# A decoder layer rebuilt as a pipeline of three chains, with folded norms and attention chunks of 64

## The chip, the cores and the metric

The kernel is written in Bass and runs on one core of one Trainium2 chip. The metric is the device time of one execution in microseconds, as a median of runs. TensorE (PE) multiplies matrices, VectorE (DVE), ScalarE (ACT) and GpSimd (POOL) work on tiles of 128 partitions, SyncE (SP) starts transfers. Each engine executes its own list of instructions in order; semaphores tie the lists together.

## The reference, cut to what matters

Everything is fp32; there are 4 batches of 256 tokens and 256 features.

```python
# attention, 16 heads of 16; the decay of a head h is r_h
h1 = layernorm(x)
q, k, v = rotary(h1 @ Wq), rotary(h1 @ Wk), h1 @ Wv
# chunks of 128 tokens, state kv of 16 x 16 per head
inter  = (q * r**(i + 1)) @ kv
intra  = ((q @ k.T) * dmask) @ v
kv     = r**128 * kv + (k * r**(127 - i)).T @ v
x1 = x + rms_norm(inter + intra, rms_w) @ Wo
# similarity with a context of 256 x 64
kv_c = ctx @ W_k.T + b_k                       # 256 x 64
sim  = (layernorm(x1) @ kv_c) @ kv_c.T / 16     # 256 x 256
x2   = x1 + softmax(layernorm(sim, eps=1e-6) * gamma + beta)
# mixture of 8 experts of 256 x 256, the best 2 by the router
h3  = layernorm(x2)
out = x2 + sum_e gate_e * (h3 @ We[e] + be[e])
```

The decay `r**n` makes chunks of any length exact: a chunk of 64 with one more state between the chunks gives the same sums.

## The kernel before, in words

A batch is worked through in three stages, all with two tiles of 128 tokens. The *front*: norm 1, transposes, the products for q, k, v, the rotation, masked scores, attention, projection, x1. The *back*: norm 2, the two products with the context keys, norm of the similarities, softmax, x2, norm 3, router logits, gates. The *experts*: eight units of a tile and two experts each (`expert_unit`, six fp32r products of 512 columns from a high and a low part of each operand), and VectorE adds each expert's product, weighted by its gate, to `acc` (`add_units`).

`passes` runs six bodies: body i has the front of batch i, the back of batch i-1 and the experts of batch i-2. Bodies 2 and 3 have all three stages and are a loop. The order of the instructions in a body is written out by hand on each engine. All products of two fp32 tiles appear in the trace as two records; fp32r products and transposes as one.

- `scores(t)`: four products of 64 rows and 512 columns for a tile. The queries are laid out in four masked copies (`qx`, made by `head_queries` on ScalarE), and VectorE multiplies each bank by the decay (`decay_scores`).
- `attend(t)`: for each head one product of 32 output rows and 128 columns, `probs` with `vpad`; for tile 1 also `state` with `qd`.
- `state_product`: one state, between the two chunks of 128.
- A norm is statistics and an aggregate on VectorE, a power of -0.5 on GpSimd (`rsqrt`), and a subtraction with multiplication on VectorE (`ln_apply`), before the transposes on TensorE.
- `keep_clock(n, ...)`: n products with the identity whose result nobody reads, 18 in all: at the start, in bodies 0 and 1, and in body 4 while the last back stage runs.
- `route`: some twenty small VectorE instructions from logits to gates.

## Time and profile before

| | |
|---|---|
| median of 3 runs | 174.38 us (174.18 to 174.51) |
| profiled execution, its own time | 174.52 us |
| its span | 172.3 us |
| TensorE busy | 152.0 us, 88% |
| VectorE busy | 123.4 us, 72% |
| ScalarE busy | 61.5 us, 36% |
| GpSimd busy | 32.2 us, 19% |

The span is what the profiler sees from the first to the last instruction; the time of an execution is 2.2 us longer. Busy time adds the intervals in which an engine has an instruction under way. Matmuls overlap in their pipeline, so a group of them can be shorter than its count times the mean of one.

### The profile page before, as it was taken

The numbers are of one execution on the slowest core, as the hardware profiler recorded it, in microseconds if no ns is written. First come the engines' busy times: TensorE is split into PE (matmuls) and PEld (weight loads), VectorE is DVE, ScalarE is ACT, GpSimd is POOL, SyncE is SP. The second block draws the span as 40 slices with busy tenths as digits, with TensorE's granted clock in tenths as the row PEclk, the third lists the DMA queues.
The fourth block names the chain that finished last, engine by engine and source line by source line (L and its number), as shares of the span: only waits on it lengthen the run. The fifth ranks groups of instructions, "written<-read, shape, count | busy, mean of one in ns | idle before, by whom it ended". The sixth has DMA issues, their size and how long they took to land.

```text
span 172.3 us, 3040 instructions
## 1 busy us (share of the span) xinstructions
PE 152.0 (88%) x981; PEld 104.0 (60%) x981; DVE 123.4 (72%) x401; ACT 61.5 (36%) x171; POOL 32.2 (19%) x53
## 2 busy tenths in 40 slices
PE   0999999799779899999779899998698899998991
PEld 0555458257436778678248787675376667636880
DVE  0523593887899889757899597668996557877762
ACT  3265846055850320537712202469203120410100
POOL 4103200314320032045200130423100204010030
PEclk9999999999999999999999999999999999999998
DMA  5999400002000000000040000000100000001001
GB/s 150 313 351 348 104 0 4 0 4 76 0 4 0 0 4 0 2 0 0 0 122 22 0 0 0 0 0 0 61 0 0 2 0 0 0 0 61 4 0 61
DMA packets 7930, 7.29 MB, mean 42 GB/s; under 512 B 2264, under 2 KB 7664, under 8 KB 7792
## 3 DMA queue, kind: packets, MB, share of 16 engines
q1 hardware_dynamic: 7424, 6.79, 12.6%
q10 hardware_dynamic: 496, 0.37, 0.8%
q8 instruction: 6, 0.10, 0.2%
q14 instruction: 4, 0.03, 0.1%
HBM read 6.11 MB, written 1.05 MB: 42 GB/s over the span
## 4 chain that ended last, share of the span: by engine, by line
PE 49%; DVE 27%; issue 7%; ACT 6%; DVEq 5%; DMA 2%; POOL 2%
PE bank L793 13%; PE ebank L793 12%; DVE probs L624 7%; PE ebank L801 4%; PE bank L841 4%; ACT qx L426 3%; DVE stats L520 2%; PE bank L923 2%; DMA cst<-in_consts 2%; PE bank L881 2%; PE bank L808 2%; DVE w_e_lo L585 2%; DVEq L521 2%; DVE norm L531 2%; POOL rs L326 2%
## 5 line engine op out<-in xcount | busy, mean ns | idle before, releaser
L624 DVE TENSOR_TENSOR probs<-bank,dec 128x512 f32<-128x512 f32 x32 | 19.8, 680 | 1.6 <-PE bank L881 1.6
L326 POOL TENSOR_TENSOR rs<-ve,nhalf 128x2 f32<-128x2 f32 x16 | 12.1, 756 | 37.1 <-DVE ve L525 37.0
L881 PE MATMUL bank<-qx,kT 64*128 64x512 f32 x64 | 18.0, 624 | 0.8 <-ACT kv L481 0.8
L801 PE MATMUL ebank<-cst 128*128 128x512 f32 (+1 forms) x22 | 11.5, 645 | 4.7 <-DMA cst<-in_consts 4.7
L558 DVE SCALAR_TENSOR_TENSOR acc<-ebank,gate,acc 128x256 f32<-128x256 f32 x26 | 11.3, 477 | 3.2 <-PE ebank L793 3.0
L793 PE MATMUL ebank<-w_e_hi,h3T_hi 128*128 128x512 f32 x40 | 13.4, 416 | 0.2 <-DVE w_e_lo L585 0.2
L426 ACT ACTIVATE qx<-bank,cst 128x256 f32<-128x256 f32 x32 | 12.6, 487 | 0.0
L558 DVE SCALAR_TENSOR_TENSOR acc<-bank,gate,acc 128x256 f32<-128x256 f32 x22 | 9.3, 478 | 4.5 <-PE bank L793 3.0
L793 PE MATMUL ebank<-w_e_hi,h3T_lo 128*128 128x512 f32 x40 | 12.5, 394 | 0.0
L793 PE MATMUL ebank<-w_e_lo,h3T_hi 128*128 128x512 f32 x40 | 12.4, 392 | 0.0
L326 POOL TENSOR_TENSOR rms_rs<-rms_ve,nhalf 128x2 f32<-128x2 f32 x4 | 3.1, 785 | 46.1 <-DVE rms_ve L768 46.1
L347 POOL TENSOR_TENSOR rot_b<-qk,cst 128x128 f32<-128x128 f32 x16 | 7.8, 505 | 19.7 <-ACT qk L400 19.7
L881 PEld LDWEIGHTS bank<-qx,kT 64*128 64x128 f32 x64 | 7.2, 185 | 6.4 <-issue 2.2
L337 POOL TENSOR_TENSOR acc<-acc,biases 128x512 f32<-128x512 f32 x4 | 5.1, 1286 | 30.2 <-DVE acc L558 30.2
L394 ACT COPY pT<-bank 128x256 f32<-128x256 f32 x8 | 2.7, 375 | 21.7 <-PE bank L808 21.7
L434 ACT ACTIVATE sqT<-bank 128x256 f32<-128x256 f32 x8 | 3.1, 383 | 18.2 <-PE bank L906 16.5
L801 PEld LDWEIGHTS ebank<-cst 128*128 128x128 f32 x22 | 4.3, 213 | 8.7 <-DMA cst<-in_consts 4.6
L906 PE MATMUL bank<-probs,vpad 128*32 128x128 f32 x256 | 9.2, 275 | 0.0
L923 PE MATMUL bank<-w_o,attT 128*128 128x256 f32 x32 | 8.9, 400 | 0.0
L808 PE MATMUL bank<-cst,norm 128*128 128x128 f32 x36 | 6.4, 301 | 2.6 <-DVE norm L531 2.5
L793 PEld LDWEIGHTS ebank<-w_e_lo,h3T_hi 128*128 128x128 f32 x40 | 7.5, 188 | 1.7
L793 PEld LDWEIGHTS ebank<-w_e_hi,h3T_lo 128*128 128x128 f32 x40 | 7.5, 188 | 1.7
(137 smaller groups left out, 321.4 us busy)
## 6 DMA issues: line engine op xcount, KB each, us to landing
w_e<-in_L_ffn_We SPq DMA_DIRECT2D x2, 1024.0 KB, 9.8
xin<-in_x SPq DMA_DIRECT2D x4, 256.0 KB, 3.8
dec<-in_decay SPq DMA_DIRECT2D x1, 1024.0 KB, 6.6
out<-outb SPq DMA_DIRECT2D x8, 128.0 KB, 1.7
cst<-in_consts ACTq DMA_DIRECT2D x1, 282.0 KB, 3.9
w_qkv<-in_L_attn_Wq SPq DMA_DIRECT2D x1, 256.0 KB, 4.4
w_qkv<-in_L_attn_Wk SPq DMA_DIRECT2D x1, 256.0 KB, 4.9
w_qkv<-in_L_attn_Wv SPq DMA_DIRECT2D x1, 256.0 KB, 5.1
```

The costliest lines, as they stand in the source:

```text
L326: nc.gpsimd.tensor_tensor(dst[:], src[:], nhalf[:], ALU.pow).then_inc(done, 1)
L347: nc.gpsimd.tensor_tensor(rot_b[:, t, :, a, :], v[:, :, 1 - a, 0:ROT], sin, ALU.mult).then_inc(s_rb, 1)
L426: o = act.activation(qx[:, t, :, k, :], bank[t][:, 0:D].rearrange("p (g n) -> p g n", g=GROUPS), ACT.Copy, scale=cst[:, C_PICK + k:C_PICK ...
L558: nc.vector.scalar_tensor_tensor(out=outb[:, t, :] if last else acc[:, t, :], in0=expert_bank(b, u)[:, (e % 2) * D:(e % 2 + 1) * D], scala ...
L624: nc.vector.tensor_tensor(probs[:, t, 4 * n:4 * n + 4, :], bank[2 + n][:].rearrange("p (h n) -> p h n", h=4), dec[:, 4 * n:4 * n + 4, :], ...
L793: mm = pe.matmul(dst, a[ka][:, c, a_cols], b[kb][:, c, b_cols], start=(n == 0 and c == 0), stop=(n == 2 and c == KC - 1))
L801: pe.matmul(dst[:, 0:cols], ident, cst[:, 0:cols], start=True, stop=True)
L808: mm = pe.transpose(banks[t][:, c * P:(c + 1) * P], norm[n][:, t, c * P:(c + 1) * P], ident)
L841: mm = pe.matmul(dst, h1T_full[:, c, cols], w_qkv[:, c, w_cols], start=(c == 0), stop=(c == KC - 1))
L881: pe.matmul(bank[2 + n][:], kT[rows, t, g, :], qx[rows, t, g, :, :], start=True, stop=True).then_inc(s_sc_ps, 1)
L906: mm = pe.matmul(bank[t][32 * q:32 * q + 32, g * P:(g + 1) * P], vpad[:, t, h, :], probs[:, t, h, :], start=(par == 0), stop=(par == 1 and ...
L923: mm = pe.matmul(bank[2 + t][:, 0:D], attT[:, t, g, :], w_o[:, g, :], start=(g == 0), stop=(g == GROUPS - 1))
```

## The change

The program is reordered and four things are computed in another way.

- **Order.** There is no loop over bodies any more. After the fronts of batches 0 and 1 and the chain of batch 0, there are bodies b = 1 to 3. A body has: attention, projection, similarity and softmax of batch b; the transposes, logits, routing and all eight expert units of batch b-1; and q, k, v, rotation, scores and states of batch b+1. The products for q, k and v of batch b+1 stand ahead of six of the eight expert units. After body 3 come the experts of batch 3. `xin`, `cin` have a buffer for each batch, `vpad`, `qd`, `state`, `kvT`, `kv`, `x2`, `h3T` have two.
- **Chunks of 64.** `scores` makes 16 products a tile of 32 rows by 64 columns of the array, with 128 columns of data; `qx` has two copies, not four; `decay_scores` reads two tiles of 128x512 per tile. `states` makes three states a batch by 32 products of 32 columns. `attend` handles both tiles: 64 products with `probs` and 24 with `state`, of 64 columns each.
- **Folded norms.** x is only centered ahead of the transposes; the factor `rs1` is applied as q, k and v leave their bank. Norm 2 is not applied at all: the centered context keys and one variance stand for it (`context_sums`, `center_x1`, `square_similarities`, `sim_variance`). Norm 3 is applied through the gates (`gate_y`), with its mean in `x1c` and its sum of squares from `square_x2` on ScalarE.
- **Dummy products.** Three calls of `keep_clock` with 256 columns at the start are left.

The core of the diff. `-` lines of the old bodies are cut; each new function shown is new or rewritten.

```diff
 @block.gpsimd
+            for b in range(B):
+                if b == 0:
+                    for t in range(TILES):
+                        rotary_cross(1, t)
+                if b + 2 < B:
+                    x_rstd(b + 2)
+                rms_rstd(b)
+                if b == 0:
+                    keys_for_states(1)
+                x1_variance(b)
+                if 0 < b < LAST:
+                    for t in range(TILES):
+                        rotary_cross(b + 1, t)
+                sim_rstd(b)
+                if 0 < b < LAST:
+                    keys_for_states(b + 1)
+                if b:
+                    add_biases(b - 1)
+                x2_rstd(b)
 @block.scalar
+            def center_x1(b, t):
+                act.wait_ge(s_nmu3, b + 1)
...
+                act.activation(x1c[:, t], x1[:, t], ACT.Identity, bias=nmu3[:, t:t + 1]).then_inc(s_x1c, 1)
+                act.activation(squares1[:, t], x1[:, t], ACT.Square, bias=nmu3[:, t:t + 1],
+                               accum_out=ssq1[:, t:t + 1]).then_inc(s_sq1, 1)
...
+            queries_keys(1, 0)
+            attention_out(0, 0)
+            attention_out(0, 1)
+            queries_keys(1, 1)
+            high_experts(1, 0)
+            head_queries(1, 0)
...
+            negate_beta()
+            context_transposed(1)
+            context_sums(1)
+            context_centered(1)
+            context_keys(1)
+            softmax_exp(0, 0)
+            softmax_exp(0, 1)
...
+            for b in range(1, B):
+                for t in range(TILES):
+                    x2_transposed(b - 1, t)
+                for t in range(TILES):
+                    square_x2(b - 1, t)
+                attention_out(b, 0)
+                attention_out(b, 1)
+                gate_exponent(b - 1)
+                if b < LAST:
+                    center_x(b + 1, 0)
+                    center_x(b + 1, 1)
+                gates_transposed(b - 1)
+                expert_biases(b - 1)
+                for t in range(TILES):
+                    x1_transposed(b, t)
+                if b < LAST:
                     for t in range(TILES):
+                        x_transposed(b + 1, t)
+                keys_product(b)
+                center_x1(b, 0)
+                center_x1(b, 1)
+                if b < LAST:
+                    context_transposed(b + 1)
+                    values(b + 1, 0)
+                    values(b + 1, 1)
+                square_similarities(b, 0)
+                square_similarities(b, 1)
+                if b < LAST:
+                    context_sums(b + 1)
+                    context_centered(b + 1)
+                    queries_keys(b + 1, 0)
+                    context_keys(b + 1)
+                    queries_keys(b + 1, 1)
+                    head_queries(b + 1, 0)
+                softmax_exp(b, 0)
+                softmax_exp(b, 1)
+                if b < LAST:
+                    head_queries(b + 1, 1)
 @block.vector
+            rotate(1, 0)
+            low_experts(0)
+            rms_variance(0)
+            residual1(0)
...
+            for b in range(1, B):
+                x2_low(b - 1, 0)
+                x2_low(b - 1, 1)
+                if b == 1:
                     low_experts(1)
+                if b + 2 < B:
+                    x_stats(b + 2)
+                route(b - 1)
+                rms_variance(b)
+                residual1(b)
+                add_experts(b - 1, 0)
+                if b < LAST:
+                    x_low(b + 1, 0)
+                    x_low(b + 1, 1)
+                sim_variance(b)
+                if b < LAST:
+                    rotate(b + 1, 0)
+                softmax_input(b)
+                if b < LAST:
+                    rotate(b + 1, 1)
+                    decay_queries(b + 1, 0)
+                add_experts(b - 1, 1)
+                residual2(b, 0)
+                residual2(b, 1)
+                if b < LAST:
+                    decay_queries(b + 1, 1)
+                    decay_scores(b + 1, 0)
+                    decay_scores(b + 1, 1)
+                add_experts(b - 1, 2)
+                if b < LAST:
+                    mask_states(b + 1)
+                add_experts(b - 1, 3)
 @block.tensor
+            def states(b):
...
+                for t, v, n in ((0, 0, 0), (0, 1, 1), (0, 2, 2), (1, STATES, 2)):
                     for g in range(GROUPS):
+                        for q in range(PAIRS):
...
+                            mm = pe.matmul(qk_bank(b, 0)[32 * q:32 * q + 32, at:at + 2 * DH],
+                                           kd[:, v, g * P + 32 * q:g * P + 32 * q + 32], pair,
...
+            def scores(b, t):
...
+                for n in range(2):
...
                     for g in range(GROUPS):
+                        for c in range(HALVES):
+                            half = slice(c * CH, (c + 1) * CH)
+                            for r in (2 * n, 2 * n + 1):
+                                rows = slice(32 * r, 32 * r + 32)
+                                mm = pe.matmul(chain[half, r, g * P:(g + 1) * P], kT[rows, t, g, half],
+                                               qx[rows, t, g, :, half], start=True, stop=True)
+            def attend(b):
...
+                            for c in range(HALVES):
+                                half = slice(c * CH, (c + 1) * CH)
+                                for q in range(PAIRS):
+                                    pe.matmul(chain[32 * q:32 * q + 32, c, cols],
+                                              vpad[b % 2][half, t, g * 8 + q * 2 + par, :], probs[half, t, q, at],
...
+                for n in range(STATES):
...
+                        for q in range(PAIRS):
+                            rows = slice(32 * q, 32 * q + 32)
+                            mm = pe.matmul(chain[rows, c, cols], state[b % 2][rows, n * GROUPS + g, :],
+                                           qd[b % 2][rows, t, g, c * CH:(c + 1) * CH], start=False,
+            def project(b, t):
...
+                if t:
+                    pe.wait_ge(s_rv, b + 1)
+            def expert(b, q, t):
...
+                elif b < LAST or q in (0, QS - 1):
+                    before = TILES * E * b + 4 * (q - 1) + 3 + t
...
+                    pe.wait_ge(s_exd, before)
+            for b in range(1, B):
+                transpose_x2(b - 1, 0)
+                transpose_x2(b - 1, 1)
+                attend(b)
+                logits(b - 1)
+                expert(b - 1, 0, 0)
+                square_sums(b)
+                project(b, 0)
+                project(b, 1)
+                transpose_gates(b - 1)
+                expert(b - 1, 0, 1)
+                bias_product(b - 1)
+                transpose_x1(b, 0)
+                transpose_x1(b, 1)
+                if b < LAST:
+                    transpose_x(b + 1, 0)
+                    transpose_x(b + 1, 1)
+                keys_product(b)
+                if b < LAST:
+                    transpose_context(b + 1)
+                    project_v(b + 1, 0)
+                    project_v(b + 1, 1)
+                similarities(b)
+                if b < LAST:
+                    context_product(b + 1)
+                    project_qk(b + 1, 0)
+                    project_qk(b + 1, 1)
+                    transpose_keys(b + 1)
+                expert(b - 1, 1, 0)
+                if b < LAST:
+                    transpose_qk(b + 1, 0)
+                expert(b - 1, 1, 1)
+                if b < LAST:
+                    transpose_qk(b + 1, 1)
+                expert(b - 1, 2, 0)
+                if b < LAST:
+                    scores(b + 1, 0)
+                    scores(b + 1, 1)
+                expert(b - 1, 2, 1)
+                if b < LAST:
+                    states(b + 1)
+                expert(b - 1, 3, 0)
+                expert(b - 1, 3, 1)
```

## Rows read from the trace of the kernel before

**Rows 1.** The page's table of busy time (us, share of the span, instructions).

```profile
PE 152.0 (88%) x981; PEld 104.0 (60%) x981; DVE 123.4 (72%) x401; ACT 61.5 (36%) x171; POOL 32.2 (19%) x53
```

**Rows 2.** Timeline of TensorE at attention: start us, length us, engine, line, operation.

```profile
55.30 1.52 PE L906 MATMUL bank<-probs,vpad 128*32 128x128 f32 x48
...
91.78 1.52 PE L906 MATMUL bank<-probs,vpad 128*32 128x128 f32 x48
...
93.11 0.40 PE L911 MATMUL bank<-qd,state 128*32 128x128 f32 x8
...
93.33 0.65 PE L906 MATMUL bank<-probs,vpad 128*32 128x128 f32 x14
...
94.23 0.61 PE L919 MATMUL bank<-onescol,sqT 128*128 128x1 f32 x4
...
127.73 1.52 PE L906 MATMUL bank<-probs,vpad 128*32 128x128 f32 x48
```

**Rows 3.** Windows: stretch, length; busy us (count) by engine, granted clock, DMA.

```profile
55.30:91.78 36.48, 33.29 (x240) 24.62 (x239) 29.99 (x100) 13.47 (x40) 7.78 (x11) 1.00 0.06 17
...
91.78:127.73 35.95, 33.01 (x239) 24.55 (x238) 28.88 (x98) 13.46 (x40) 7.39 (x11) 1.00 0.02 8
...
169.00:172.30 3.30, 0.00 (x0) 0.00 (x0) 1.05 (x3) 0.00 (x0) 0.00 (x0) 0.79 0.24 79
```

**Rows 4.** Chain of work that ended last: start us, us, what.

```profile
22.36 0.44 PE bank L890 x4
...
22.81 1.92 PE bank L881 x8
...
30.66 0.89 DVE x L776 x2
...
36.24 0.59 PE bank L957 x8
...
101.14 2.75 PE bank L793 x12
...
150.71 0.50 DVE x L617
```

**Rows 5.** Timeline of TensorE, products of `keep_clock`.

```profile
4.65 2.93 PE L801 MATMUL ebank<-cst 128*128 128x512 f32 x4 [4.65 <-DMA cst<-in_consts]
...
16.75 1.98 PE L801 MATMUL ebank<-cst 128*128 128x512 f32 x4
```

**Rows 6.** Groups of weight loads by shape: busy us, mean ns, idle before.

```profile
L911 PEld LDWEIGHTS bank<-qd,state 128*32 128x32 f32 x64 | 2.3, 110 | 0.0
...
L957 PEld LDWEIGHTS bank<-pT,kv 128*64 128x64 f32 x32 | 1.7, 136 | 0.9 <-issue 0.9
...
L890 PEld LDWEIGHTS bank<-vpad,kd 128*128 128x128 f32 x16 | 2.2, 191 | 0.5 <-issue 0.5
```

**Rows 7.** Timeline of VectorE: routing, four additions, the last additions.

```profile
93.32 0.18 DVE L632 TENSOR_REDUCE lg<-ebank 128x16 f32<-128x32 f32 x1
...
96.10 0.18 DVE L665 TENSOR_TENSOR gate_parts<-gate,gate_parts 128x16 fp32r<-128x16 f32 x1
...
146.05 1.66 DVE L558 SCALAR_TENSOR_TENSOR acc<-ebank,gate,acc 128x256 f32<-128x256 f32 x4
...
169.19 0.86 DVE L558 SCALAR_TENSOR_TENSOR outb<-ebank,gate,acc 128x256 f32<-128x256 f32 x2
```

**Rows 8.** Timeline of ScalarE: copies of queries, a pass with a sum.

```profile
114.60 0.22 ACT L418 ACTIVATION_READ_ACCUMULATOR ez<-zb,nmax 128x1 f32 x1
...
116.71 1.58 ACT L426 ACTIVATE qx<-bank,cst 128x256 f32<-128x256 f32 x4
```

**Rows 9.** The page's costliest groups, VectorE and GpSimd: busy us, mean ns.

```profile
L624 DVE TENSOR_TENSOR probs<-bank,dec 128x512 f32<-128x512 f32 x32 | 19.8, 680 | 1.6 <-PE bank L881 1.6
...
L326 POOL TENSOR_TENSOR rs<-ve,nhalf 128x2 f32<-128x2 f32 x16 | 12.1, 756 | 37.1 <-DVE ve L525 37.0
...
L347 POOL TENSOR_TENSOR rot_b<-qk,cst 128x128 f32<-128x128 f32 x16 | 7.8, 505 | 19.7 <-ACT qk L400 19.7
```

1506 lines of the change are left out of this document (798 added, 708 removed).

## The prediction

> **What bounds the kernel now.** I read the page's busy table first [rows 1]: TensorE is busy for 152.0 of 172.3 us, VectorE for 123.4. Then the places where one product recurs, the attention product `probs x vpad`: it starts at 55.30, 91.78 and 127.73 us [rows 2]. So the span falls into four stretches: 55.3 us until the second batch attends, two bodies of 36.5 and 36.0, and 44.6 to the end. The windows cut at these points [rows 3] say what fills a body: 33.3 and 33.0 us of TensorE, 30.0 and 28.9 of VectorE, 13.5 of ScalarE. A body is TensorE's work plus 3 us of holes. The chain of waits changes hands between TensorE and VectorE all the way [rows 4]. A change that shortens norms on VectorE, ScalarE or GpSimd gains little in a body unless TensorE's own time falls too, so I count TensorE first.
>
> **TensorE's work in one body.** An fp32 product is two records in the trace, an fp32r product one.
> Weight loads of 32, 64 and 128 columns last 110, 136 and 190 ns [rows 6]: 26 or 27 ns more for each 32 columns, on a fixed 83. I read this as loads that stream one after the other, 27 ns per 32 columns. The pace of the small products fits: 48 records of 128 columns run from 91.78 to 93.11, 27.7 ns each, and 8 records of the state product until 93.33, 27.5 ns each [rows 2].
> - `attend` now takes 80 records in 2.45 us (91.78 to 94.23) [rows 2]. After: 64 products with `probs` and 24 with `state`, 176 records. The columns per record halve (64 for 128), the weight loads double. At 27.5 ns: 4.84 us, +2.4.
> - `states` replaces 4 records of 0.44 us in all [rows 4] by 32 products, 64 records: 1.76 us, +1.3.
> - `scores`: now 16 records, 1.92 us a tile [rows 4], 3.84 a batch. After: 64 records a batch, each with a 64-column load, 53 ns by the step of [rows 6]: 3.4 us, -0.4. The nearest row with such loads, the key product, took 0.59 us for 8, 74 ns each [rows 4]: 4.7 us, +0.9. I take 53, as the four tiles of the array are all distinct.
> - q, k, v, expert units (2.75 us for two [rows 4]), context and routing products are the same instructions in other places: 0.
>
> Sum: 33.2 + 3.3 = 36.5 us of TensorE in a body, already its whole present length. The floor of the unseen cost is that time goes with columns alone: half of 27.6, 13.8 ns a record. That would make attend 2.4, states 0.9 and scores (half of 3.84) 1.9 us: 31.7 in all. The ceiling is the key product's 74 ns for scores. The nearest rows to `attend` and `states` are at 27.5, with the same 32-column loads, so I take that.
>
> The Trainium skill speaks to this (TensorE: Matmul & The Clock Gate, "Wait — 56ns, not 53.3ns?"): start-to-start of matmuls never falls below about 25 ns, however few columns. By it attend would be 4.4 us (an estimate), not 4.84, and halving the columns buys nothing. No run here yet shows 64-column records.
>
> **What leaves the other engines.** Masked scores: 4 of 0.68 us a tile become 2, about -2.5 us on VectorE [rows 9]; `qx` 4 copies a tile become 2, -1.5 us on ScalarE (four in 1.58 [rows 8]). The norms lose statistics and normalizing passes on VectorE and return as ScalarE passes with a sum (`center_x1`, `square_similarities`, `square_x2`, `context_sums`): some 0.36 us back to back plus 0.22 for a sum [rows 8]. VectorE falls to about 26 us a body, ScalarE rises from 13.5 [rows 3] to about 20. Neither is the bound as a sum. They matter as links of the chain.
>
> **The chain through a body after.** I count from the start of `transpose_x2(b-1)` on TensorE, in each queue's new order.
> 1. Transposes to 0.5, attend to 5.35, `logits` to 6.6, one expert unit to 8.0.
> 2. `route(b-1)` starts at 6.65 and takes 3.0 us now [rows 7] plus 0.2 for `gate_y`: 9.8. `rms_variance(b)` is queued behind it on VectorE: 9.95. GpSimd's root 0.8 [rows 9], `residual1` 0.89 [rows 4]: x1 at 11.7. `project(b, 1)` waits for `rms_variance` as well.
> 3. TensorE goes through projection, gates, the second expert unit, bias: 13.0; x1 transposed 13.45. ScalarE is then busy without a break: biases, pT and h1T 15.05, pkvT 15.35, `center_x1` 17.2, ctxT 17.6, values 18.5, squares 19.7, context 21.05, q and k of both tiles 22.6.
> 4. `sim_rstd(b)` is behind both `rotary_cross(b+1, t)` on GpSimd. The second needs q and k of tile 1: 22.6 + 1.0 + 0.8 [rows 9] = 24.4, 4.7 us after the squares were done. `softmax_input` to 26.3; `rotate(b+1, 1)` is queued behind it: 27.1. So `transpose_qk(b+1, 1)` leaves TensorE idle for about 2 us.
> 5. `add_experts(b-1, 1)` to 29.0 (four in 1.66 [rows 7]), x2 at 30.35. Expert unit (2,0) waits for its bank until 28.6. Then scores 1.7 and 1.8, expert unit, states 1.8, two expert units: 39.5.
>
> A body is thus 39.5 us: TensorE's 34 or so by sum of steps, and 5.5 of holes. Now: 36.2 on the mean.
>
> **Before the bodies.** The first product starts 0.6 us earlier (no root ahead of the centred x). From there the front of batch 1 is laced into batch 0's. `attend(0)` ends at about 33.5. `low_experts(0)` on VectorE needs `high_experts(1, 0)`, which ScalarE does only after `attention_out(0)`, and `rms_variance(0)` is queued behind it: x1 of batch 0 at about 39.5, now 31.55 [rows 4]. In exchange the second front is nearly through. `softmax_input(0)` waits for `negate_beta` on ScalarE, scores of batch 1 for `context_keys(1)`. The second attend starts at 55.6; now 55.3. No gain.
>
> **The end.** Batch 3 attends, with the eight units of batch 2 as filler. Expert unit (2,0) waits from 18.8 to 22.5 for `add_experts(2, 1)`, queued behind `softmax_input(3)`. x2(3) is ready at 24.25, 23.75 after attend's start (now 23.5 [rows 2, 4]), but its transposes are queued behind three more units: 28.1. Then, without a third norm ahead of them, transposes, parts and logits to 31.3. Eight units and routing to 43.0, last addition 44.2, and 2.25 us from there to the end as now (170.05 to 172.3 [rows 7]): 46.5. Now 44.6 [rows 2].
>
> **Sum.** 55.6 + 39.5 + 39.5 + 46.5 = 181.1 us; the profiled execution took 174.52 for a span of 172.3, so 2.2 lie outside: 183.3. The median of the runs is 0.14 below the profiled one. I say 183.
>
> **The rivals.**
> - *Small products at array pace (0.20).* Two row halves and four column groups abreast would put a 64-column record at 13.8 ns. 896 small records lie on the path (176 + 64 at the start, 240 in each body, 176 at the end): 896 x 13.7 = 12.3 us less, and about 3.0 less for scores: 168.0, faster. It decides where 8.8 us are won: 3.0 on scores and a pace of 21 ns. For it: half the columns. Against: the stepping load time [rows 6] and that 32 columns of weights never went faster than 27 ns [rows 2]. The Trainium skill (TensorEngine Tiling, "Theoretical Speedup") promises up to 16 times for both dimensions small, which is this case's best end.
> - *The lacing hides the holes (0.12).* Expert units absorb steps 4 and 5, and a body is its 36.5 us of work: 6 less, 177.3; with 3 to 5 more from the start, 172 to 175.
> - *The clock falls (0.13).* The first four dummy records (two of 512 and two of 256 columns) took 2.93 us, four of 512 later 1.98, so the first ran at the lower of the two levels, 1.2 and 2.4 GHz [rows 5]; and with TensorE idle over the last 3.3 us the granted clock averaged 0.79 [rows 3]. The change leaves 3 of the 18 dummy calls. TensorE is nearly idle from about 46 to 54 us, and for 3.7 us in the last body. At half clock for some 5 us behind each: 3 more at the end, 2 more at the start, 188.
> - *The forecast itself (0.55)*: 177 to 187.
>
> **Numbers.** Faster by over 0.2% (about what this kernel's runs can tell from no change): the first rival's 0.20 and 0.05 of the second's, 0.25. Within: 0.03. Slower: 0.72. The range takes in the floor of the small records and the clock case: 168 to 190; the forecast's own range is 177 to 187.
>
> **What would show it.** Right: 64-column records 25 to 28 ns apart; attend near 4.8 us; its starts 39 to 40 us apart; `sim_rstd` ending GpSimd's wait after the rotary terms; TensorE waiting for `rotate(b+1, 1)`; `rms_variance(0)` behind `low_experts`. Wrong: attend under 3 us; a body under 36; the second attend before 50 us; a granted clock of half after the holes.

## The result, and the profile after

The changed kernel takes 184.49 us (median of four runs, 183.99 to 185.95); the kernel before took 174.44 beside it. The ratio is 1.0583, with an interval from 1.0515 to 1.0651: slower. The forecast was 183.0. Some executions of the kernels below ran at a lower mean clock than others of the same kernel; the intervals leave them out and the medians don't, so where the two part, single runs are given.

The total fits. It does not follow that its terms do, so I go through the trace in the order in which the forecast was made. First the page of the changed kernel: busy time by engine, two of its rows by slices (a digit is the busy share, or the granted clock in tenths, of a fortieth of the span), and the queue that loads instructions (packets, MB, share).

```profile
PE 144.8 (79%) x1767; PEld 108.8 (60%) x1767; DVE 96.1 (53%) x322; ACT 73.7 (40%) x228; POOL 38.0 (21%) x70
...
PE   1996696976269989947999989577978974779991
...
PEclk9999579579855999996699999975699999696999
...
q8 instruction: 14, 0.23, 0.5%
```

TensorE has less to do than before (144.8 us for 152.0 in [rows 1]), though part of it ran at the lower clock, and VectorE is 22% lighter. Neither bounds the kernel: TensorE is idle for 37 us of 182. The row of the clock has seven dips, each with or just behind a slice in which TensorE's digit is 7 or less.

The windows, cut at the attentions as in [rows 3] (stretch, length; busy us and count for PE, PEld, DVE, ACT, POOL; granted clock; DMA), then seven short ones:

```profile
0.00:55.50 55.50, 39.10 (x551) 27.87 (x552) 24.00 (x73) 28.98 (x78) 14.58 (x32) 0.82 0.33 100
55.50:95.03 39.53, 34.32 (x443) 26.20 (x442) 24.60 (x81) 16.37 (x55) 9.41 (x15) 0.87 0.01 2
95.03:133.78 38.75, 34.41 (x443) 26.09 (x442) 21.49 (x72) 16.51 (x55) 8.06 (x14) 0.87 0.03 8
133.78:182.20 48.42, 36.92 (x333) 28.64 (x332) 26.06 (x99) 11.81 (x43) 5.95 (x9) 0.93 0.05 17
44.00:48.00 4.00, 0.68 (x6) 0.29 (x2) 1.33 (x5) 3.22 (x10) 0.88 (x2) 1.00 0.00 0
80.00:84.00 4.00, 2.31 (x10) 1.63 (x10) 3.93 (x11) 1.72 (x5) 1.84 (x2) 0.91 0.01 4
116.00:120.00 4.00, 1.22 (x8) 0.55 (x6) 3.97 (x13) 2.22 (x8) 2.10 (x4) 1.00 0.00 0
152.00:156.00 4.00, 2.20 (x7) 1.78 (x8) 3.93 (x12) 1.10 (x4) 1.29 (x1) 0.86 0.00 0
83.20:90.10 6.90, 5.98 (x73) 4.14 (x72) 5.08 (x10) 0.00 (x0) 0.86 (x1) 0.51 0.01 2
49.10:59.30 10.20, 7.58 (x238) 6.06 (x239) 7.53 (x17) 4.53 (x15) 1.55 (x2) 0.50 0.01 2
120.80:131.00 10.20, 9.28 (x141) 6.51 (x140) 6.71 (x14) 0.00 (x0) 0.97 (x1) 0.50 0.01 2
```

The stretches are 55.5, 39.5, 38.8 and 48.4 us, where the forecast had 55.6, 39.5, 39.5 and 46.5. But the bodies of before ran at a granted clock of 1.00 throughout [rows 3], and these at 0.87. In the last three windows it is half, 1.2 of 2.4 GHz, and two of the three begin within 1.1 us of the end of a window in which TensorE was busy for only 0.68 and 1.22 of 4 us (48.0 to 49.1, 120.0 to 120.8); the third begins inside one with 2.31 (83.2).

Next the small products, on TensorE's timeline (start us, length us, line, operation, records). The third attention is at the full clock, the second at half of it; the last shows a stop:

```profile
55.50 2.04 PE L1176 MATMUL chain<-probs,vpad 64*32 64x64 f32 x128
57.48 1.29 PE L1185 MATMUL chain<-qd,state 32*32 32x64 f32 x40
59.31 0.31 PE L1185 MATMUL chain<-qd,state 32*32 32x64 f32 x8 [0.55 <-issue]
...
90.57 0.76 PE L1106 MATMUL front<-vpad,kd 128*32 128x32 f32 x64
...
95.03 1.48 PE L1176 MATMUL chain<-probs,vpad 64*32 64x64 f32 x128
96.45 0.87 PE L1185 MATMUL chain<-qd,state 32*32 32x64 f32 x48
...
133.78 1.48 PE L1176 MATMUL chain<-probs,vpad 64*32 64x64 f32 x128
135.20 0.52 PE L1185 MATMUL chain<-qd,state 32*32 32x64 f32 x20
137.09 0.64 PE L1185 MATMUL chain<-qd,state 32*32 32x64 f32 x28 [1.37 <-issue]
```

From 95.03 to 96.45, where the next form begins, 128 records take 1.42 us: 11 ns each, not the forecast's 27.5. At half the clock it is 15.5 ns (55.50 to 57.48). The states' 64 records take 0.76 us, 12 ns. Attention as a whole lasts 2.2 us at the full clock (95.03 to 97.25), where the forecast had 4.84: the largest term of its count for TensorE was wrong by more than a factor of two. In the first body, at half the clock and with a stop, the same attention still took 4.1 us (55.50 to 59.56).

What stood in its place? The waits of step 4, in the first body, are there (an entry in brackets is idle time before the instruction, and what ended it):

```profile
73.15 0.16 DVE L850 SCALAR_TENSOR_TENSOR sim_ve<-ssq,ve 128x2 f32<-128x2 f32 x1 [3.75 <-ACT squares_sim L586]
...
75.07 0.99 POOL L363 TENSOR_TENSOR rot_b<-qk,cst 128x128 f32<-128x128 f32 x2 [3.68 <-ACT qk L494]
...
76.40 0.82 POOL L363 TENSOR_TENSOR rot_b<-qk,cst 128x128 f32<-128x128 f32 x2 [0.33 <-ACT qk L494]
...
77.17 0.69 POOL L348 TENSOR_TENSOR sim_rs<-sim_ve,nhalf 128x2 f32<-128x2 f32 x1
...
78.00 0.88 DVE L859 SCALAR_TENSOR_TENSOR zg<-chain,sim_rs,gam 128x256 f32<-128x256 f32 x2 [1.40 <-POOL sim_rs L348]
...
80.92 0.66 PE L1090 MATMUL front<-cst,qk 128*128 128x128 f32 x4 [2.07 <-DVE qk L794]
...
82.74 1.60 DVE L873 SCALAR_TENSOR_TENSOR x<-ez,rsum,x1c 128x256 f32<-128x256 f32 x1
82.78 1.28 POOL L409 TENSOR_TENSOR acc<-acc,biases 128x512 f32<-128x512 f32 x1 [1.21 <-DVE acc L943]
```

`sim_ve` is ready at 73.3 and GpSimd begins its root at 77.17, behind the cross terms of both tiles; TensorE then stands idle 2.07 us for `rotate(2, 1)`. The same hole comes again at 118.62 (2.05 us). The clock falls at 83.2, 2.3 us after the first of them ended, and at 120.8, 2.2 us after the second. The last two lines were in nobody's forecast: VectorE's x2 instruction takes 1.60 us instead of 0.48 while GpSimd adds the biases.

### The profile page after: what moved, and what is told of

The parts are those of the page before. It is cut to its first block, busy times and chain, and to the rows that moved or that the text cites. A ratio compares the mean times of both kernels' runs of the same rounds, so it can differ in the third digit from the quotient of the medians.

```text
span 182.2 us, 4515 instructions
## 1 busy us (share of the span) xinstructions
PE 144.8 (79%) x1767; PEld 108.8 (60%) x1767; DVE 96.1 (53%) x322; ACT 73.7 (40%) x228; POOL 38.0 (21%) x70
## 4 chain that ended last, share of the span: by engine, by line
PE 59%; ACT 14%; issue 10%; DVE 9%; POOL 3%; DMA 2%; POOLq 1%; DVEq 0%; ACTq 0%
PE ebank L1037 24%; PE chain L1205 5%; PE chain L1158 5%; PE chain L1176 3%; DVE acc L943 2%; PE chain L1185 2%; ACT squares_x L575 2%; PE front L1257 2%; PE chain L1195 2%; PE front L1044 2%; POOL rot_b L363 2%; DMA cst<-in_consts 2%; ACT qx L516 2%; PE front L1029 2%; PE chain L1025 2%
## 5 line engine op out<-in xcount | busy, mean ns | idle before, releaser
L1037 PE MATMUL ebank<-w_e_hi,h3T_hi 128*128 128x512 f32 x56 | 22.2, 481 | 5.3 <-DVE acc L943 4.6
L943 DVE SCALAR_TENSOR_TENSOR acc<-ebank,gate_y,acc 128x256 f32<-128x256 f32 x40 | 17.4, 478 | 11.3 <-PE ebank L1037 11.3
L1037 PE MATMUL ebank<-w_e_lo,h3T_hi 128*128 128x512 f32 x56 | 20.2, 445 | 0.0
L1037 PE MATMUL ebank<-w_e_hi,h3T_lo 128*128 128x512 f32 x56 | 19.7, 437 | 0.0
L1037 PEld LDWEIGHTS ebank<-w_e_hi,h3T_hi 128*128 128x128 f32 x56 | 10.3, 216 | 9.2 <-DVE acc L943 6.1
L1158 PE MATMUL chain<-qx,kT 32*64 32x128 f32 x256 | 10.8, 429 | 3.5 <-DVE probs L826 3.1
L826 DVE TENSOR_TENSOR probs<-chain,dec 128x512 f32<-128x512 f32 x16 | 10.3, 686 | 5.9 <-PE chain L1158 5.9
L1158 PEld LDWEIGHTS chain<-qx,kT 32*64 32x64 f32 x256 | 7.8, 213 | 6.5 <-issue 6.5
L372 POOL TENSOR_TENSOR kd<-qk,cst 128x256 f32<-128x256 f32 x16 | 10.0, 644 | 5.6 <-DVE qk L794 5.6
L1205 PE MATMUL chain<-w_o,attT 128*128 128x256 f32 x32 | 10.3, 467 | 0.0
L873 DVE SCALAR_TENSOR_TENSOR x<-ez,rsum,x1c 128x256 f32<-128x256 f32 x8 | 7.2, 905 | 0.3
```

The lines of the kernel that those rows point to most:

```text
L372: o = nc.gpsimd.tensor_tensor(kd[:, n].rearrange("p (h d) -> p h d", h=H), qk[:, t, D:].rearrange("p (h d) -> p h d", h=H), kdec[:, v].uns ...
L826: nc.vector.tensor_tensor(probs[:, t, rows], chain[:, rows, 0:D], dec[:, rows], ALU.mult).then_inc(s_sc, 1)
L873: nc.vector.scalar_tensor_tensor(out=x2[b % 2][:, t, :], in0=ez[:, t], scalar=rsum[:, t:t + 1], in1=x1c[:, t, :], op0=ALU.mult, op1=ALU.ad ...
L943: nc.vector.scalar_tensor_tensor(out=outb[:, t, :] if last else acc[:, t, :], in0=expert_bank(b, q, t)[:, (e % 2) * D:(e % 2 + 1) * D], sc ...
L1037: mm = pe.matmul(dst, a[ka][:, c, a_cols], b[kb][:, c, b_cols], start=(n == 0 and c == 0), stop=(n == 2 and c == KC - 1))
L1158: mm = pe.matmul(chain[half, r, g * P:(g + 1) * P], kT[rows, t, g, half], qx[rows, t, g, :, half], start=True, stop=True)
```

## Experiments

The theory after the result: the holes of step 4, of the start and of the end cost twice, once as idle time and once more because the clock falls behind them; the small products are cheap, and their price has nothing to do with the time. Rivals: the holes alone; the small products after all; the supply of instructions, that is TensorE standing still until its next instructions have been loaded.

**1. Fill the holes.** TensorE computes products that nobody reads (512 columns of fp32 into a free bank; two records, 0.96 us), 19 of them in the places where it waits. Nothing else changes.

```
+            def fill(n, dst=None):
+                for _ in range(n):
+                    pe.matmul((chain[:, 2] if dst is None else dst)[:, 0:512], ident, w_qkv[:, 0, 0:512],
+                              start=True, stop=True)
...
                 if b < LAST:
+                    fill(2)
                     transpose_qk(b + 1, 1)
+                else:
+                    fill(3)
                 expert(b - 1, 2, 0)
```

> The changed kernel with dummy products (identity times a weight tile, 512 columns, 0.43 us a record at the full clock) in the holes of TensorE: before transposes and scores that wait, in the stretch before the second attend, and in the last body; nobody reads their result. Theory clock: the changed kernel ran TensorE at 1.2 GHz for about 48 of 182 us, behind its holes, and the pieces of work in these stretches took some 14 us longer than the same pieces elsewhere; with the holes filled the mean granted clock is above 0.97 and the time falls from 184.5 to 172 to 177. Rival waits: the low clock costs only time in which TensorE would wait anyway; the clock rises but the time stays within 182 to 185.

Measured: median 174.20 (172.50 to 176.77), ratio to before 0.99 (0.986 to 0.9939); the runs behind the ratio took 172.6 and 172.5 us, at a mean clock of 0.987 and 0.990, where the changed kernel has 0.869. With 18 us of work added it is 12 us faster than the changed kernel, and 1% faster than the kernel before. The clock rival had the right cause. The supply of instructions is not what was won back: the stops with no releaser inside the attentions add up to 3.4 us in this version's trace (1.88 and 1.54) and to 3.5 in the changed kernel's (1.57, 0.55 and 1.37).

**2. Take two waits out of the queues.** GpSimd takes the root of the similarity's variance ahead of the cross terms; VectorE does the softmax's input ahead of both rotations.

```
+                sim_rstd(b)
                 if 0 < b < LAST:
                     for t in range(TILES):
                         rotary_cross(b + 1, t)
-                sim_rstd(b)
...
-                if b < LAST:
-                    rotate(b + 1, 0)
                 softmax_input(b)
                 if b < LAST:
+                    rotate(b + 1, 0)
                     rotate(b + 1, 1)
```

> The changed kernel with GpSimd's root for the similarities ahead of the rotary terms of the next batch, and VectorE's softmax input ahead of both rotations. Theory order (step 4 of the prediction): in bodies 1 and 2 the softmax input starts at once behind the squares instead of 4.7 us later, the hole of 2 us before the transposes of q and k of tile 1 goes or halves; 178 to 182, of it 2 to 3 us for each body, if the clock stays as it is. Rival: the rotation is now late instead, the hole moves to the transposes of tile 0, and the time stays within 183 to 186.

Measured: median 175.18 (174.29 to 181.96), ratio 1.0033 (0.9993 to 1.0074), 9.3 us under the changed kernel. The expectation was too small, since it priced the idle time alone. The root now begins 0.1 us after its input (timeline of this version):

```profile
74.50 0.16 DVE L850 SCALAR_TENSOR_TENSOR sim_ve<-ssq,ve 128x2 f32<-128x2 f32 x1 [3.74 <-ACT squares_sim L586]
74.74 0.69 POOL L348 TENSOR_TENSOR sim_rs<-sim_ve,nhalf 128x2 f32<-128x2 f32 x1 [2.00 <-DVE sim_ve L850]
```

The mean clock rose to 0.931: with the hole of each body smaller, the two clock falls in the bodies did not come. Two short moves are worth nearly as much as the dummy work.

**3. Both.** The edits of 1 and 2 together.

> Both edits. If clock and order are separate costs, the gains add: 167 to 173, below the kernel before. If the hole was the cause of the low clock, the sum is less than the parts: 172 to 176.

Measured: median 170.03, ratio 0.9655 (0.9596 to 0.9714), from runs of 169.05 and 167.52. The time lies in the range that the expectation gives for gains that add, but that range was built on smaller gains. Those measured, 11.9 and 9.3, would add up to 163.3; they don't add, since both take back the same clock. The orders are worth some 4 us on top of the filling. Windows of this version:

```profile
0.00:52.31 52.31, 40.52 (x567) 25.42 (x568) 23.95 (x73) 29.16 (x80) 14.56 (x32) 1.00 0.36 106
52.31:89.53 37.22, 34.66 (x448) 25.96 (x448) 25.19 (x81) 15.73 (x54) 9.69 (x15) 0.95 0.01 2
89.53:123.63 34.10, 33.09 (x449) 24.60 (x448) 21.89 (x72) 16.23 (x55) 8.53 (x14) 1.00 0.03 10
123.63:167.30 43.67, 37.82 (x343) 28.08 (x342) 25.89 (x99) 11.77 (x43) 5.94 (x9) 0.99 0.06 19
```

A body at the full clock is 34.1 us, two short of the 36.0 of before. TensorE is busy for 33.1 of them, of which three dummies are 2.9: the body's own work is about 30.2 us. This version is the base of what follows.

**4. The small products twice.** On the changed kernel the state products are issued two times, 64 records more in each of four batches.

```
-                for t, v, n in ((0, 0, 0), (0, 1, 1), (0, 2, 2), (1, STATES, 2)):
+                for t, v, n in ((0, 0, 0), (0, 1, 1), (0, 2, 2), (1, STATES, 2)) * 2:
```

> The changed kernel with the 32 products of the states issued twice for each batch (the second set repeats the first): 64 records more a batch, three of the four batches on the path. By the prediction's price of 27.5 ns a record: 3 x 1.76 = 5.3 us more, 189.8. By the pace that the trace of the changed kernel shows for its small products, 11 to 16 ns: 3 x 0.7 to 1.0 = 2 to 3 us more, 186.5 to 187.5. Rival supply: long runs of small instructions stop TensorE for 0.5 to 1.6 us each, put down to issue, and more of them give more such stops: 188 or more at an unchanged pace between the stops.

Measured: median 183.66 (182.46 to 187.6), ratio 1.0514 (1.0468 to 1.056): no rise, where all three expectations had one.

```profile
25.40 1.48 PE L1106 MATMUL front<-vpad,kd 128*32 128x32 f32 x128
...
42.97 1.20 PE L1106 MATMUL ebank<-vpad,kd 128*32 128x32 f32 x116
45.89 0.32 PE L1106 MATMUL ebank<-vpad,kd 128*32 128x32 f32 x12 [1.73 <-issue]
```

128 records in 1.48 us: 11.6 ns, so the forecast's pace is refuted a second time. A stop of 1.73 us with no releaser has appeared inside them, where the changed kernel has none; with those inside the attentions the stops add up to 6.0 us, for 3.5. So the supply rival is right about the stops. It is wrong about the time, because the mean clock is higher (0.906): TensorE ran at half clock for 34 us instead of 48. I have not tested why.

**5. The start.** On the base of 3: ScalarE converts `high_experts(1, 0)` before `attention_out(0)`, GpSimd takes the RMS root before `x_rstd(2)`, VectorE does `sim_variance(0)` before `decay_queries(1, 1)`, and the context's copy goes ahead of a conversion.

```
+            high_experts(1, 0)
             attention_out(0, 0)
             attention_out(0, 1)
             queries_keys(1, 1)
-            high_experts(1, 0)
...
             rotate(1, 1)
-            decay_queries(1, 1)
             sim_variance(0)
+            decay_queries(1, 1)
             softmax_input(0)
```

> Base: the version with filled holes and the new queue orders (median 170.03 us, its profiled run 169.05, attentions at 26.1, 52.3, 89.5 and 123.6 us). Theory: ahead of the loop three more waits are only waits in queues: `rms_variance(0)` stands on VectorE behind a `low_experts` piece that waits 4.12 us for ScalarE's `high_experts(1, 0)`, so that `project(0, 1)` waits 1.35 us; `sim_variance(0)` stands behind `decay_queries(1, 1)`, which comes 1.4 us after the squares are ready; and the context's copy stands on ScalarE behind a 1.06 us conversion. With all three moved, the second attention should start 2 to 3 us sooner (49.3 to 50.3) and the median be 167 to 168. Rival: TensorE stops for its instructions in the attention products anyway (1.87 and 1.53 us there); if that supply is what bounds this stretch, the stops grow by what the waits lose, and the time stays within 1 us (169 to 171).

Measured: four runs of 166.06, 168.1, 171.26 and 171.64, at mean clocks from 0.996 down to 0.956 (the base: 167.52 to 171.79). In the two profiled runs, 169.05 and 166.06, the second attention starts 1.6 us sooner (50.69) and the third and fourth 3.0 sooner (86.51, 120.62): 1.6 from the waits, less than expected, and 1.4 because the clock fall of the base behind its second attention (56.9 to 60.3 us) did not come. The stops in the attentions stayed at 1.87 and 1.54 us, so the rival falls, but with runs 2 us apart the gain in time is not settled by this experiment alone.

**6. The last body.** On the base of 3: an expert unit in place of a dummy in front of `keys_product`, the additions of unit pairs 1 and 2 ahead of the softmax and of x2, the gates transposed two units sooner at the end. All five dummies of the last body and behind it are out.

```
-                if b == LAST:
-                    fill(1)
+                if b == LAST:
+                    expert(b - 1, 1, 0)
                 keys_product(b)
...
+                if b == LAST:
+                    add_experts(b - 1, 1)
                 sim_variance(b)
                 softmax_input(b)
```

> Same base (170.03). Theory: the end is long because in the last body the expert units are queued where they wait for VectorE's additions, and these stand behind the softmax; the fills (four of 0.5 us) and the waits before `expert(2, 2, 0)` and `expert(2, 3, 0)` (0.86 and 1.40 us) go, and the 1.3 us by which VectorE waits for the biases at the end. With the units in the gaps, the additions ahead of the softmax, and the gates transposed two units sooner, the end from the last attention (43.7 us in the base) should be 38 to 40, the median 165 to 167. Rival: the last x2 becomes late (the softmax now stands behind four additions, 1.7 us, and GpSimd's addition of the biases falls on it), and TensorE waits before its transposes with a hole long enough to lower the clock: 168 to 171.

Measured: median 167.35 (166.19 to 167.61), ratio 0.9574 (0.9494 to 0.9653). The end is 42.4 us from the last attention, not 38 to 40: the rival came in part. (The expectation also counts a dummy at 0.5 us; it lasts 0.96.) Two lines say where the rest went:

```profile
138.51 1.27 DVE L943 SCALAR_TENSOR_TENSOR acc<-ebank,gate_y,acc 128x256 f32<-128x256 f32 x3 [2.82 <-PE ebank L1040]
...
149.03 0.36 PE L1260 MATMUL front<-w_r_hi_lo,h3T_hi 128*128 128x16 f32 x2 [1.78 <-DVE h3T_lo L881]
```

The additions delay `sim_variance` to 139.69, and TensorE waits 1.78 us for the low part of x2, queued behind four additions more.

**7. q, k, v behind two of the units.** On the base of 3, this undoes the lead of q, k and v that the section on the change describes: in bodies 1 and 2 the next batch's context product, q, k and key transposes come after units (1, 0) and (1, 1).

```
                 similarities(b)
+                expert(b - 1, 1, 0)
+                expert(b - 1, 1, 1)
                 if b < LAST:
                     context_product(b + 1)
                     project_qk(b + 1, 0)
                     project_qk(b + 1, 1)
                     transpose_keys(b + 1)
-                expert(b - 1, 1, 0)
-                if b < LAST:
                     transpose_qk(b + 1, 0)
-                expert(b - 1, 1, 1)
```

> Same base (170.03): in bodies 1 and 2 the next batch's context product, q and k, and key transposes stand behind the units (1, 0) and (1, 1), that is ahead of four expert units instead of six. This undoes, on this base, the last phrase of the change's name. If the lead is needed: the way from q, k to the next attention (copy 0.69, cross terms 0.76, rotation 0.43, transposes, 1.2 us of copies, scores, two decays of 1.3) no longer hides behind the four units of 5.6 us that are left, and each of the two bodies grows by 1 to 3 us: 172 to 176. Rival: the lead is not needed, as the softmax and x2 set the next attention's start: 169.5 to 170.5.

Measured: median of ten runs 175.57 (172.56 to 181.35), ratio 0.9953 (0.989 to 1.0017) against the base's 0.9655, so 3% or some 5 us slower. The second body, at the full clock in both, is 36.2 us (94.42 to 130.59) against 34.1; the first, 42.6 against 37.2, also has a stretch of 10 us at half clock. So the lead itself is worth 2.1 us a body, and the rest of the 5 comes with the clock. The lead is needed, and it is a gain of the change that the total hides.

**8. The biases apart.** On the base of 3, GpSimd's addition of the biases waits until both tiles of x2 are written.

```
                 pool.wait_ge(s_exd, TILES * E * b + 8)
+                if b < LAST:
+                    pool.wait_ge(s_x2, TILES * (b + 2))
```

> Base: the version with filled holes and new queue orders (170.03; its profiled run 169.05). GpSimd's addition of the expert biases (1.29 us) waits until both tiles of x2 are written, instead of running while VectorE computes the first. Theory: the two engines hold each other up when both work on SBUF alone: VectorE's x2 instruction, 1.61 us while the addition runs, comes down to 0.48 in all three bodies; the addition then falls on the decays of the scores, which read PSUM, and if these are held up as well (0.43 more or up to 1.2 more in each body) nothing is won: 168 to 171. Rival: the 1.6 us have another cause (the length of a wait inside the record, the operands of x2 itself): x2 stays at 1.6 us with no GpSimd work beside it, and the time rises by the wait for the biases, 171 to 173.

Measured: 169.46 to 174.63, median 173.5, where the base has 167.52 to 171.79: nothing won that these runs could show, as three of the four ran at a mean clock of 0.970 or less. But the mechanism shows in the trace. The first group of the base, the second of this version (busy us, mean ns):

```profile
L873 DVE SCALAR_TENSOR_TENSOR x<-ez,rsum,x1c 128x256 f32<-128x256 f32 x8 | 7.3, 908 | 0.3
```

```profile
L828 DVE TENSOR_TENSOR probs<-chain,dec 128x512 f32<-128x512 f32 x16 | 10.3, 684 | 3.9 <-PE chain L1159 3.9
...
L875 DVE SCALAR_TENSOR_TENSOR x<-ez,rsum,x1c 128x256 f32<-128x256 f32 x8 | 3.9, 485 | 0.3
```

All eight x2 instructions now last 0.48, without GpSimd beside them. In the first body GpSimd's addition (85.24 to 86.52) lies beside `qd`, which reads PSUM and takes its usual 0.49 for two. So the holding up goes with instructions of VectorE that have both inputs in SBUF. It is not on the path in the second body, which is at the full clock in both versions: 34.11 us here (94.53 to 128.64) and 34.10 in the base.

**9. A rest inside attention.** On the base of 3, two dummy products stand between the 128 and the 48 small products of each attention.

```
+                fill(2)
                 for n in range(STATES):
                     t, c = divmod(n + 1, HALVES)
```

> Same base (170.03): two dummy products of 512 columns (0.94 us) stand in each of the four attentions between the 128 products with probs and the 48 with the states. The base has stops of 1.87 and 1.53 us with no releaser in the first two attentions' state products and none in the last two. If such a stop is TensorE running out of instructions that are being fetched, time in which it works on few long instructions lets the fetch catch up: the two stops shrink by about 0.9 us each, the last two attentions get 0.9 us longer, and the sum is near 170 to 172. Rival: the stop has another cause that goes with the place (a wait that the trace doesn't name): both stops stay at 1.5 to 1.9 us, and the whole is 3.8 us longer, 173 to 174.

Measured: median 171.69 (171.35 to 172.22), ratio 0.9849 (0.9775 to 0.9923). The second attention of the base, then of this version:

```profile
52.31 1.47 PE L1175 MATMUL chain<-probs,vpad 64*32 64x64 f32 x128 [0.43 <-issue]
53.72 0.54 PE L1184 MATMUL chain<-qd,state 32*32 32x64 f32 x24
55.79 0.54 PE L1184 MATMUL chain<-qd,state 32*32 32x64 f32 x24 [1.53 <-issue]
```

```profile
52.28 1.48 PE L1175 MATMUL chain<-probs,vpad 64*32 64x64 f32 x128 [0.43 <-issue]
53.68 1.98 PE L1294 MATMUL chain<-w_qkv,cst 128*128 128x512 f32 x4
55.60 0.87 PE L1185 MATMUL chain<-qd,state 32*32 32x64 f32 x48
```

The two rests last 1.92 us (53.68 to 55.60), twice what the expectation says. Both stops, 1.87 and 1.53 us, are gone, and the last two attentions, which had none, are 1.9 and 1.8 longer. That is what instructions on their way would do: the stop vanishes when the engine is given something long to do in the meantime, which a wait tied to the place would not. It wins nothing, since 1.92 us of work replaced 1.87 of standing still, and the second attention starts at 52.28 for 52.31.

The packed traces settle it. They hold each packet of the instruction queue q8 (16 KB) with its time. In the changed kernel packets landed at 29.58, 57.97 and 135.70 us, and TensorE resumed at 30.93, 59.31 and 137.09, that is 1.35, 1.34 and 1.39 us later. It is the same in all 25 stops of 0.5 us or more inside runs of small records in these traces: TensorE resumes 1.20 to 1.57 us after a packet has landed. In the third attention of the changed kernel (95.03 to 97.25) no packet lands, and there is no stop.

**10. All of it.** Prologue as in 5; rests in the first two attentions; and in the last body two unit pairs on free banks, two additions ahead of the softmax instead of four, the low part of x2 before the last additions.

```
+            if b == LAST - 1 and q == 2 or b == LAST and q == 1:
+                return chain[:, 1 + t]
+            if b == LAST and q in (0, 3):
+                return chain[:, 3 * t]
+            return ebank[t]
...
+                if b < LAST:
+                    add_experts(b - 1, 3)
             x2_low(LAST, 0)
             x2_low(LAST, 1)
+            add_experts(LAST - 1, 3, 0, 2)
             route(LAST)
+            add_experts(LAST - 1, 3, 2, 4)
```

> Both edits that measured a gain on the base, with the last body's miss mended. The prologue's orders gave 3 us of the profiled run; the rests of 0.94 us between the 128 and the 48 small products go only into the first two attentions, where they took away stops of 1.87 and 1.53 us. In the last body four additions no longer stand ahead of `sim_variance` (1.2 us late before) nor ahead of `x2_low` (TensorE waited 1.78 us for it); two expert units there and two of the last batch write to free banks, so that they wait for no addition. Expected: the end from the last attention 38 to 40 us where the base has 43.7 and the first version of this edit 42.4; the other three stretches 24 + 35.5 + 34; in all a median of 160 to 164. Rival: VectorE, with some 15 us of additions, routing and one 1.3 us wait for GpSimd behind the last x2, now sets the end and it stays at 41 or more: 164 to 167.

Measured: median 162.17 (161.58 to 163.28), ratio 0.9286 (0.9218 to 0.9354): 7% faster than the kernel before. Its last three stretches:

```profile
51.61:87.81 36.20, 35.17 (x452) 25.28 (x453) 25.00 (x81) 15.26 (x51) 9.23 (x15) 1.00 0.01 2
87.81:121.91 34.10, 33.08 (x449) 24.54 (x449) 21.87 (x72) 16.26 (x55) 8.55 (x14) 1.00 0.03 10
121.91:161.50 39.59, 34.24 (x333) 26.34 (x332) 25.75 (x99) 11.88 (x43) 5.95 (x9) 1.00 0.06 21
```

The end is 39.6 us, in the expected range, and the rival, with 41 or more, did not come.

**11. Without the rests.** As 10, with the rests and one dummy of the start taken out and the context's keys and the exponentials ahead of a conversion on ScalarE.

> Base: the version with all edits (median 162.17 us; profiled run 163.28, attentions at 25.96, 51.61, 87.81, 121.91 us). A rest of two dummy products turned out to last 1.92 us, as much as the stop that it replaced (1.87 and 1.53 us), so the rests should have won nothing. Without them the stops should come back at about their old length and the time stay within 0.5 us on that account. The other edit is in the stretch before the second attention: one of the three dummy products ahead of the context product goes (0.96 us), and ScalarE copies the context's keys and takes the exponentials ahead of a 1.03 us conversion, behind which TensorE waited 0.86 us. Expected from this: the second attention 1 to 1.8 us sooner. In all 160 to 161.5. Rival: the hole in front of the context product is only as long as the dummy work made it and the clock falls behind the shorter filling: 162 to 164.

Measured: profiled run 159.88, the fastest execution of all, with the second attention at 48.56 for 51.61: 3 us sooner, more than the 1 to 1.8 expected, as the clock fall at 46.4 to 49.8 us of version 10 is gone too. The stops are back at 1.49 and 1.44. But the six runs spread from 159.88 to 165.58 (median 163.19, ratio 0.9341, 0.9288 to 0.9395), their mean clock from 1.000 down to 0.955. The same program holds its clock in some executions and not in others, as version 3 did (0.987 down to 0.966); whether the missing filling is the reason is not tested. The median is no better than that of 10, and which of the two is faster stays open.

## Why the prediction came out right, and where it was not

The time, 183 for 184.49, and the sign were right. The argument was half right. Its terms, in its own order:

- **Attend, states, scores.** Mis-sized, and the largest error. Attend lasts 2.2 us, not 4.84; states 0.76, not 1.76; scores 0.65 and 1.1 for the two tiles (timeline of version 3), 1.75 and not 3.4. For four attentions and three of the others that is 10.6 + 3.0 + 5.0 = 18.6 us too much. The step that failed was the reading of [rows 6] as loads that stream one after the other, 27 ns per 32 columns. It fails for the old shape of the load too: the records of `states` have tiles of 128 rows by 32 columns, as the 27.5 ns records of [rows 2] had, and run 12 ns apart. What they have less of is data, 32 columns for 128, so the 27.5 ns were not the price of the load. The first rival, small products at array pace, had 13.8 ns; measured are 11 to 12, in the changed kernel and in version 4, and 17 on the tiles of 32 x 32. It had the right mechanism and the wrong result, 168.0, because it left the clock and the waits as they were. The Trainium skill (TensorE: Matmul & The Clock Gate, "Wait — 56ns, not 53.3ns?") gives 25 ns as the least distance between two starts; for records of 64 columns on tiles of 64 x 32 and 32 x 32 it does not hold here, and the measured 11 and 17 ns decide. The prediction also has two sums for TensorE's work in a body, 36.5 us and "34 or so by sum of steps", and does not reconcile them. Measured, without dummies and at the full clock, it is 30.2 (version 3), near the 31.7 that it gave as the floor.
- **The chain through a body** looks right in the first body, to within about a microsecond at every point that I compared. From the start of the x2 transposes at 54.42 us, x1 came at 11.0 (forecast 11.7), the variance of the similarities at 18.7 (squares 19.7), `rotate(b+1, 1)` at 26.4 (27.1), x2 at 30.5 (30.35), the next transposes at 40.1 (39.5). The hole of step 4 was forecast at about 2 us and is 2.07 and 2.05. The order of the waits is as forecast, but the times agree partly by luck: here attend took 4.1 us, near the forecast's 4.84, only because the clock was at half and TensorE stopped. In the second body, at the full clock until 120.8, the same points come earlier, counted from 94.50 us: x1 at 8.6, the variance at 16.3, the rotation at 24.1, x2 at 28.1. That is 2.2 to 3.4 us ahead of the forecast. The 10 us at half clock behind them then brought the next transposes to 38.8.
- **Before the bodies.** x1 of batch 0 at 39.5, forecast and measured, behind `low_experts(0)` and `high_experts(1, 0)`; second attention at 55.50 for 55.6. Version 5 confirms this wait. The agreement in time is again partly luck, since TensorE ran at half clock for 20 of these 55.5 us.
- **The end.** The wait of unit (2, 0) is there, 2.60 us at 153.80, and in versions 6 and 10, which move those additions and drop the dummies there, the stretch is 42.4 and 39.6 us, for 43.7 in the base (10 also gives units free banks). 48.4 us, not 46.5, with 6.8 of them at half clock.
- **The clock.** The rival with 0.13 had the largest cost that the forecast itself left out. It named two places and 5 us; the clock was at half in seven stretches, 48 us in all, and the difference to version 1 is 12 us. It was priced as if a fall needed a long rest at the start or the end, while the forecast's own holes of 2 us in each body were enough to bring it.
- **The lacing** (0.12) was wrong as stated: the units did not absorb steps 4 and 5. Version 7 shows what the lead is worth all the same, 2.1 us in a body at the full clock and some 5 in all with the clock.
- **Not in the forecast:** TensorE standing without instructions, 1.57, 0.55 and 1.37 us in the changed kernel; and VectorE held up for 1.1 us three times. (A fourth wait with no releaser, 0.77 us at 82.35, is another thing: it stands before unit (2, 0), where the second body has 0.72 us put down to an addition. It is the wait for a bank in step 5.)

A rough tally, worked out and not measured as such: 183.3, less 18.6 for the small products, plus 12 for the clock, plus 3.5 for the stops, is 180.2; the profiled run took 183.99. The held-up instructions are not on the path in the one body where version 8 can be compared, so they are not added. Some 4 us of the account stay open, and the terms need not add up, as the 12 us were measured on another version. What is shown is the pace, the clock's 12 us, the waits in the queues (9.3 us with the clock that they bring down, some 4 without) and the stops. The forecast came out by luck: the small products, priced 18.6 us too dear, stood in for the clock and the stops, 15.5 us that it left out.

So where did the gain of the change go? The change does shorten the work: at the full clock and with two queue orders mended a body takes 34.1 us instead of 36.0. It was lost to waits in the queues of GpSimd, VectorE and ScalarE, and to the clock, which fell behind them.

## What to carry to other kernels

When a change lightens every engine and leaves holes on TensorE, price each hole twice: its length, and the stretch at half clock behind it. Then look in the queues of the light engines for a short instruction that stands behind one waiting for another chain; moving two such instructions was worth 9 us here. Filling the holes with products that nobody reads shows in one experiment whether the clock is the cause, before anything is rebuilt.

## What the runs showed of the hardware

- Small tiled products are issued 11 to 12 ns apart: 11 with 64 columns of data on tiles of 64 x 32 (128 records in 1.42 us), 12 with 32 columns on tiles of 128 x 32 (64 in 0.76). Those with 64 columns on tiles of 32 x 32 take 17 ns (48 in 0.80). With 128 columns on tiles of 128 x 32 it was 27.5 [rows 2]. At half clock the first take 15.5, not twice as long.
- In dense runs of such records TensorE stops for 0.5 to 2.1 us with no releaser, for instance after 116 records (version 4) or after 152 (the changed kernel's first attention), while its third attention, 176 records, has no stop. Each of the 25 stops ends 1.20 to 1.57 us after a packet of the instruction queue has landed. The kernel has 1767 records on TensorE, before 981, and that queue moved 14 packets and 0.23 MB, before 6 and 0.10.
- VectorE is held up by GpSimd for the length of an addition (1.28 us) when both of its inputs lie in SBUF, and not when one is in PSUM. In version 6 the scaling of the similarities (PSUM, 140.75) kept its 0.88 us for two beside the addition, and the next instruction (SBUF) took 0.62 instead of 0.41:

```profile
140.58 1.30 POOL L409 TENSOR_TENSOR acc<-acc,biases 128x512 f32<-128x512 f32 x1
...
140.75 0.88 DVE L859 SCALAR_TENSOR_TENSOR zg<-chain,sim_rs,gam 128x256 f32<-128x256 f32 x2 [0.91 <-POOL sim_rs L348]
...
141.54 0.62 DVE L863 CUSTOM_DVE_ANT_0 zb<-zg,nbet 128x256 f32<-128x256 f32 x1
```

  The Trainium skill (SBUF — State Buffer, "SBUF: two separate sides") says this of the port pair that the two engines share; the traces agree, with 1.60 for 0.48 us. The page gives the pair to whichever instruction starts first. By the rows VectorE's starts 0.04 us ahead of GpSimd's (82.74 and 82.78) and is still the one that waits, so this part is not confirmed here.
- The clock can fall behind a stop of 1.5 us as well, but need not: in version 3 it is at half from 56.9 to 60.3 us, right behind the stop of 1.53, and in version 9, without that stop, it is not (mean clock 1.000). In the profiled run of version 5 the same stop, 1.54 us before 54.16, has no fall behind it.
